# Stacks cleared by VectorE and ScalarE, and the last attention's scores and weighing taken two units at a time

## The reference

```python
# first attention (L0 a), on the layernorm of x: 16 heads of 8, causal
scores = causal_kern[distance] + qm[..., :, None] + km[..., None, :] + 0.15 * (qc @ kc.T) / sqrt(8)
ctx = softmax(where(causal, scores, -1e9)) @ v
...
# last attention (L1 b), on the layernorm of x: 16 heads of 64, one key and value head for all
sim = (q * 64 ** -0.5) @ k.T + rel_emb[bucket(distance)] * 64 ** 0.5      # [4, 16, 1024, 1024]
attn = softmax(where(later_key, -inf, sim))
out = (attn @ v).reshape(4, 1024, 16 * 64) @ Wout + bout
```

## Time and profile before

| what | us |
|---|---|
| median of three runs (3611.07 to 3620.83) | 3611.9 |
| the profiled execution, its own time | 3624.34 |
| its span, first to last instruction | 3622.6 |
| first attention's projection stage, about | 12.8 to 170 |
| last attention's rounds | 2551 to 3371 |
| PE / DVE busy in the span | 3095.8 (85%) / 2363.0 (65%) |

### The profile page before, as it was taken

How to read it: one execution, slowest core, us unless ns; L and a number is a source line. 1 busy time by engine, 2 the same in 40 slices (tenths; PEclk the granted TensorE clock), 3 DMA queues, 4 the chain that set the end, 5 groups by cost and what they waited for, 6 DMA issues and landing times. The chain is left out here.

```text
span 3622.6 us, 67291 instructions
## 1 busy us (share of the span) xinstructions
PE 3095.8 (85%) x25109; PEld 1695.5 (47%) x25109; DVE 2363.0 (65%) x5080; ACT 1838.2 (51%) x3304; POOL 945.5 (26%) x655
## 2 busy tenths in 40 slices
PE   2487999984769999797599978999899999999899
PEld 1223444432347555573222225775355555555676
DVE  2557888872855555564599963225889898889222
ACT  1222666662246233363289962443566666666344
POOL 0004999993100223000000000000222323222100
PEclk8676999997979899896589987999899999999999
DMA  3402333321042000132522210005634334332000
GB/s 82 157 28 66 109 113 114 110 71 35 10 146 94 1 1 1 48 126 77 159 57 69 64 49 19 1 1 181 131 94 104 100 95 104 91 90 73 21 10 12
DMA packets 215996, 264.12 MB, mean 73 GB/s; under 512 B 45243, under 2 KB 164503, under 8 KB 213356
## 3 DMA queue, kind: packets, MB, share of 16 engines
q1 hardware_dynamic: 215709, 260.27, 24.2%
HBM read 204.15 MB, written 56.55 MB: 72 GB/s over the span
## 5 line engine op out<-in xcount | busy, mean ns | idle before, releaser
L1182 POOL TENSOR_TENSOR l0aa_e<-l0aa_e,l0aa_et 128x1024 f32<-128x1024 f32 (+1 forms) x288 | 512.0, 1817 | 46.9 <-ACT l0aa_e L1325 46.9
L2535 ACT ACTIVATE l1ba_sg<-l1ba_sg,l1ba_mn 128x128 f32<-128x128 f32 (+7 forms) x512 | 394.6, 775 | 194.2 <-DVE l1ba_mn L2587 193.1
L2596 DVE STREAM_TRANSPOSE l1ba_pT<-l1ba_sg 128x1024 f32<-128x1024 f32 (+3 forms) x344 | 367.2, 1067 | 42.9 <-PE l1ba_pO L2495 33.0
L2587 DVE CUSTOM_DVE_ANT_0 l1ba_sg<-l1ba_pS,l1ba_tab 128x128 f32<-128x128 f32 (+7 forms) x512 | 368.2, 743 | 34.9 <-PE l1ba_pS L2475 23.1
L1353 DVE TENSOR_REDUCE l0aa_low<-l0aa_pP 128x8 f32<-128x1024 f32 x288 | 343.3, 1220 | 69.9 <-PE l0aa_pP L1206 65.8
L319 PEld LDWEIGHTS f_pY<-l_w,f_hT 128*128 128x128 f32 x2048 | 268.3, 192 | 123.5 <-issue 118.6
L2495 PE MATMUL l1ba_pO<-l1ba_pT,l1ba_v 32*64 32x256 f32 x9216 | 314.3, 387 | 4.6 <-ACT l1ba_y L2550 4.6
L2952 ACT ACTIVATE l1aa_e<-l1aa_e 128x1536 f32<-128x1536 f32 x192 | 284.4, 1483 | 49.1 <-DVE l1aa_e L2993 28.2
L2475 PE MATMUL l1ba_pS<-l1b_k,l1ba_qs 64*128 64x384 f32 (+3 forms) x1024 | 256.6, 581 | 52.1 <-DVE l1ba_mn L2587 38.1
L2423 POOL TENSOR_TENSOR l1ba_co<-l1ba_co,l1ba_rb 128x1024 f32<-128x1024 f32 x64 | 151.4, 2365 | 563.4 <-ACT l1ba_co L2543 492.5
L282 ACT ACTIVATE f_hT<-f_pH,l_b 128x512 f32<-128x512 f32 x256 | 173.9, 687 | 237.4 <-PE f_pH L311 237.2
(11 more groups left out here) (401 smaller groups left out, 5047.4 us busy)
## 6 DMA issues: line engine op xcount, KB each, us to landing
f_wB<-l0f_weights SPq DMA_DIRECT2D x16, 2048.0 KB, 7.1
l1ba_rb<-l1b_rdd SPq DMA_DIRECT2D x64, 512.0 KB
l0aa_et<-l0a_table SPq DMA_DIRECT2D x16, 1536.0 KB, 7.6
l1b_qd<-l1bp_part SPq DMA_DIRECT2D x64, 256.0 KB, 2.3
l1ba_qs<-l1b_qd SPq DMA_DIRECT2D x64, 256.0 KB
l0aa_et<-l0a_table SPq DMA_DIRECT2D x16, 512.0 KB, 8.1
l1ba_tab<-l1b_table SPq DMA_DIRECT2D x32, 256.0 KB, 5.3
l1ba_qs<-l1b_qd SPq DMA_DIRECT2D x64, 128.0 KB
```

Source lines behind the costliest of these rows:

```text
L1182: nc.gpsimd.tensor_tensor(es, es, t, ALU.mult).then_inc(multiplied, heads)
L2535: nc.scalar.activation(row, row, ACT.Exp, bias=mn[:, r % 2, i + k:i + k + 1], scale=-1.0, accum_out=den[:, r % 2, i + k:i + k + 1]).then_i ...
L2587: nc.vector.tensor_tensor_reduce(row, scores, bias, 1.0, 3e38, ALU.add, ALU.min, mn[:, r % 2, h:h + 1]).then_inc(m_done, 1)
L2596: nc.vector.transpose(pT[r % 2][:, i * width(r):(i + heads) * width(r)], sg[:, n % RING, 0:heads * width(r)]).then_inc(t_done, 1)
```

## The change

**At the start.** `fill_stacks` keeps the three transfers of ones and loses the four of zeros. Instead DVE clears rows 32 to 127 of `qs` in the first block (two memsets), ACT copies zeros to rows 32 to 63 of `ks` there and to rows 64 to 127 at the head of the projection's block; SP waits for the latter (`cleared`) before `fill_stacks`. x is loaded in two parts, and the first block doesn't wait for the second. DVE's wait for the weights stands behind the first layernorm (which also waits for `h0_ready`, that PE raises after its own wait for the weights, as before).

**In the last attention.** Nothing but S is due at an even n (counted over all 344 units); at an odd n, behind S(n), stands all that was due at n - 1 and n. The weighing of block 2 moves from the one unit of block 0 to u0' to u2' of the next group, that of block 1 to u3' and u4', that of block 0 to u5' and u6', and the projections of blocks 3, 2 and 1 to u3', u5' and u7'. The turned rows of block 2, 1 and 0 lie side by side in `pT1`, `qs` is used by the parity of the block, and block 7's queries lie in the last seventh of `pT1` (`q7`).

```diff
@@ fill_stacks
-    for dst, name in ((qs[51:54], "minus_ones"), (ks[48:51], "ones"), (ks[MAX_ROWS:MAX_ROWS + 3], "ones"),
-                      (qs[54:MAX_ROWS], "zeros"), (qs[MAX_ROWS + 3:], "zeros"), (ks[54:MAX_ROWS], "zeros"), (ks[MAX_ROWS + 3:], "zeros")):
+    for dst, name in ((qs[51:54], "minus_ones"), (ks[48:51], "ones"), (ks[MAX_ROWS:MAX_ROWS + 3], "ones")):
@@ l0a_project, SP and ACT
+            sp.wait_ge(cleared, 1)
             fill_stacks(sp, D, qs, ks, filled)
...
+            clear_stack(nc, x, ks[64:P]).then_inc(cleared, 1)
             act.wait_ge(w_in, 16 * NW)
@@ attention_strips
+    END = N + 10
+    def turned(r):
+        return {2: (1, 0), 1: (1, 3 * HG * P), 0: (1, 5 * HG * P)}.get(block_of(r), (1 - block_of(r) % 2, 0))
+    def turned_free(r):
+        return r - {7: 3, 6: 1, 1: 2, 0: 5}.get(block_of(r), 1)
+    def next_group(r):
+        return FIRST[r + block_of(r) + 1]
+    def weigh_steps(r):
+        if block_of(r) <= 2:
+            at, steps = {2: (0, 3), 1: (3, 2), 0: (5, 2)}[block_of(r)]
+            return next_group(r) + at, steps
+        return FIRST[r + 1] + 3, FIRST[r + 2] - FIRST[r + 1] - 1
+    def project_step(r):
+        if 1 <= block_of(r) <= 3:
+            return next_group(r) + {3: 3, 2: 5, 1: 7}[block_of(r)]
+        return FIRST[r + 3] + 2 if r + 1 < ROUNDS else N + 8
+    def due(n):
+        return (n - 1, n) if n % 2 else ()
@@ attention_strips, PE (ACT's loop is changed alike)
-            for n in range(FIRST[ROUNDS + 2] + 3):
+            for n in range(END):
                 if n < N:
                     scores(n)
-                for r in range(ROUNDS):
-                    if n == FIRST[r + 3] + 2:
-                        project(r)
-                for r in range(ROUNDS):
-                    first, units = FIRST[r + 1] + 2, FIRST[r + 2] - FIRST[r + 1]
-                    if units > 1:
-                        first, units = first + 1, units - 1
-                    if first <= n < first + units:
-                        weigh(r, (n - first) * pairs(r) // units, (n - first + 1) * pairs(r) // units)
+                for m in due(n):
+                    for r in range(ROUNDS):
+                        if m == project_step(r):
+                            project(r)
+                    for r in range(ROUNDS):
+                        first, units = weigh_steps(r)
+                        if first <= m < first + units:
+                            weigh(r, (m - first) * pairs(r) // units, (m - first + 1) * pairs(r) // units)
```

More of the change, by code:

```diff
@@ L1403, in _, with l0_attn_a @@
                     add_table(n)
-def l0_attn_a(nc, D, x, C, tag, out=None):
+def l0_attn_a(nc, D, x, C, tag, first, out=None):
     with ExitStack() as ctx:
@@ L1550, in _ @@
                 dve.sem_inc(sent[par], 16 * SENDS)
+            layernorm(0, 0)
             dve.wait_ge(w_in, 16 * NW)
-            layernorm(0, 0)
             with dve.Fori(0, BATCH) as b:
@@ L1555, in _ @@
                     g = b * 2 + par
+                    if par:
+                        dve.wait_ge(C["x_rest"], 16)
                     layernorm(g + 1, 1 - par)
@@ L2355, in load_queries @@
             def load_queries(r):
-                if r >= 2:
-                    sp.wait_ge(s_done, FIRST[r - 1])
+                slot = block_of(r) % 2
+                if block_of(r) == U - 1:
+                    if r >= U:
+                        sp.wait_ge(pv_done, r - U + 2)
+                    dst, done = q7, q7_in
+                else:
+                    before = {6: 2, 5: 4}.get(block_of(r), 2)
+                    if r >= U or block_of(r) < 5:
+                        sp.wait_ge(s_done, FIRST[r - before + 1])
+                    dst, done = qs[:, slot], q_in[slot]
                 b, hg = group_of(r)
@@ L2402, in _ @@
                     spread_sums(r - 1)
-                if r + 2 < ROUNDS:
+                if r + 2 < ROUNDS and block_of(r + 2) != U - 1:
                     load_queries(r + 2)
+                if u == 3 and r + 4 < ROUNDS:
+                    load_queries(r + 4)
                 if u == 1 and r + U < ROUNDS:
@@ L2550, in projected @@
                 nc.scalar.activation(y[:, r % 2], pO[BANKS[0]][:, 0:DIM], ACT.Copy).then_inc(y_out, 1)
[L2552 to L2558, removed]
+            for n in range(END):
+                for m in due(n):
+                    for r in range(ROUNDS):
+                        if m == project_step(r):
+                            projected(r)
+                    for r in range(ROUNDS):
+                        if m == out_step(r):
+                            out(r)
                 if n < N:
@@ L3076, in build @@
         C.update(ident=ident, mhalf=mhalf, ident16=ident16, flip=flip)
[L3077 to L3091, removed]
+        C["x_rest"] = ctx.enter_context(nc.semaphore("x_rest"))
@@ new lines, in first, with _ @@
+        def first(qs, ks):
+            with nc.Block() as block:
+                @block.sync
+                def _(sp):
+                    rows = D["x"].rearrange("(b p) d -> p b d", p=P)
+                    sp.dma_start(x[:, GROUP_BLOCKS:3 * GROUP_BLOCKS, :], rows[:, 0:2 * GROUP_BLOCKS, :]).then_inc(loaded, 16)
+                    sp.dma_start(ident[:], D["identity"]).then_inc(loaded, 16)
+                    sp.dma_start(ident16[:], D["identity16"]).then_inc(loaded, 16)
+                    sp.dma_start(flip[:], D["flip"]).then_inc(loaded, 16)
+                    sp.dma_start(x[:, 3 * GROUP_BLOCKS:GROUP_BLOCKS + BLOCKS, :], rows[:, 2 * GROUP_BLOCKS:, :]).then_inc(C["x_rest"], 16)
+                    sp.wait_ge(loaded, 66)
+                @block.scalar
+                def _(act):
+                    act.wait_ge(padded, 1)
+                    clear_stack(nc, x, ks[32:64])
+                @block.vector
+                def _(dve):
+                    nc.vector.memset(x[:, 0:GROUP_BLOCKS, :], 0.0).then_inc(padded, 1)
+                    nc.vector.memset(x[:, GROUP_BLOCKS + BLOCKS:, :], 0.0).then_inc(loaded, 1)
+                    nc.vector.memset(mhalf[:], -0.5).then_inc(loaded, 1)
+                    nc.vector.memset(qs[32:64], 0.0)
+                    nc.vector.memset(qs[64:P], 0.0)
@@ L3092, in build @@
         we = nc.dram_tensor("l0f_weights", (2, 8, GROUP), F32, kind="Internal").ap()
-        l0_attn_a(nc, D, x, C, "l0a")
+        l0_attn_a(nc, D, x, C, "l0a", first)
         with ExitStack() as stages:
```

42 lines of the change are left out of this document (29 added, 13 removed).

## The result

| | before | after |
|---|---|---|
| median of 12 runs, us | 3619.34 (3607.12 to 3632.73) | 3588.28 (3579.71 to 3601.69) |
| profiled execution / its span | 3624.34 / 3622.6 | 3586.44 / 3584.7 |
| first rows of the table stage (`l0at_pU`), behind the projection | 176.3 | 126.0 |
| last rows of the table stage (`l0at_pN`) | 268.6 | 207.7 |
| first scores of the last attention | 2551.3 | 2489.5 |

The ratio is 0.9923, 95% interval 0.9906 to 0.9941: 31 us faster in the medians, not 63. In the two profiles the changed kernel is 50.3 us ahead at the start of the table stage, 60.9 at its end, 61.8 at the last attention, and only 37.9 behind it. The start did what was forecast; the last attention, forecast at -12, took 24 us more (818.7 to 842.6 us from its first scores to its last copy to `y`).

A forecast was written before the change was run, and what follows sets the result against it. It took a start stall behind SP's clears as wholly on the path, and neither DVE nor PE alone as bounding the last attention. 3624.3 - 51 - 12 = 3561 profiled, or 3611.9 - 63 = 3549 us median; range 3515 to 3582.

The forecast's parts named there:

- The start: Up to the projection's end: no stall behind the clears, table load moved, first block longer; -51 us, bounds -40 and -54.
- the last attention, forecast at -12: Whole last attention: -5.5 us at group ends, -8 inside groups, +1.5 for the drain after the last scores.
- Changes of kind: PE in the last attention: 219 fewer switches between kinds of work at 0.19 us each, -41.6 us of PE's time.
- a handover to ACT that S used to cover: PE's uncovered waits in the last attention: 26 more for y at 0.52 us, 29 more for out at 0.70; +33.8 us.
- The walk of the ends: Step-by-step pricing from scores of u42 to lows of u8': even ends 25.0 us (-3.1), odd ends 30.4 (+2.3).
- Inside a group: From u16 to u42: fewer switches of kind against bare handovers; -1.0 us a group, -8 in all, bounds -3 and +1.5.
- The bounds: Last attention: -28 to +8 us with inner bounds alone, -35 to +20 with all ends even-like or odd-like.
- the handovers outweigh it: Last attention: odd ends and pairs with a projection lose 1 us more each, 38 us; 3566 to 3591; chance 0.18.
- The fourth rival: Last attention: the second unit's scores hold PE, DVE waits in each of 172 pairs; slower than before; chance 0.04.
- From the profile to the median: Whole kernel: the profiled execution lies 12.4 us over the median of the runs, so 3561 became 3549 us.

The follow-up runs named there:

- e1: The start of the changed kernel with the last attention of the kernel before: 3563 us, ratio 0.9844 to before.
- e4: The changed kernel with units paired only where neither has a projection, all others unit by unit: 3524 us, ratio 0.9747 to before.
- e6: The changed kernel's PE order (all units paired) with ACT's order from e4: 3575 us, ratio 0.9879 to before.
- e5: The changed kernel's ACT order (all units paired) with PE's order from e4: 3589 us, ratio 0.9924 to before.
- e12: e4 with ACT taking a unit's exponentials ahead of the copies to y and out due at it: 3595 us, ratio 0.9932 to before.
- e2: The changed kernel with the pairing alone undone, the moved weighing kept: 3545 us, ratio 0.9804 to before.
- e9: e4 with the weighing of block 1 whole at u4' and of block 0 whole at u6': 3533 us, ratio 0.9766 to before.
- e10: e4 with POOL's copies of the next group's table rows taken earlier: 3532 us, ratio 0.9757 to before.
- e11: e9 and e10 together, with rows 32 to 63 of qs cleared by POOL instead of DVE: 3506 us, ratio 0.9697 to before.

## Why the prediction was wrong

- **The start: right.** Forecast -51, measured -50.3 at the end of the projection, -55 in e1's median. ACT's group 2 began 50.7 us earlier. In this is that the first layernorm began 2.1 us later (21.70 for 19.56), because two issue gaps of 1.3 us were not in the price of the memsets, and that the table load gave its 1.3 us back. The first block ended near 15, not by 14 us. The rule of the Trainium skill, "VectorE: DVE Perf Modes", section "Zero memsets can be issued as uint32 (trn2)", that zeros go out as words, agrees with the row (6144 for 12288 elements, as the order had shown). Its one cycle per element gave an estimate of 6.4 us; the row has 5.18, and 6.5 with the gap ahead, so that its end at 14.8 is near the 15.0 of the row for another reason than its own.
- **Changes of kind: 28.0 us of the 41.6.** So much less was PE busy in the last attention, where no record is missing. (Over the whole span it was 43.1 us less, 3095.8 to 3052.7, which looks like the forecast by luck: 10.7 of them are the table stage's, which ran at the lower clock for longer before.) In e4, with 452 runs of equal kind for 607, PE was busy 29.8 us less, which is 0.19 for each of 155. The further 64 changes that the changed kernel saves, all at pairs with a projection, brought nothing (730.7 us for e4's 728.8); why is not shown.
- **The failed step: "Against it stands a handover to ACT that S used to cover", at 0.52 and 0.70 us, 33.8 in all.** The count was about right (36 bare handovers to y and 32 to out, of which 32 and 31 were waits), the price was that of an idle ACT. The rows it came from the earlier trace rows stand where nothing was queued ahead of y and out. In a pair the exponential of its first unit is ahead, and at the first even end the eight of u42, where PE stood 2.25 us for y ahead of its W at 2585.12. Measured: 1.18 for an out, 0.77 for a y, 61.2 us in all, 52.3 more than before. So the net of -41.6 + 33.8 = -8 was -28.0 + 51.9 = +24, the idle time being all of PE's.
- **A right price would not have been enough.** e6 has bare handovers at about the forecast's price, 34.4 us in all and 25.5 more than before, and stands 51 us over e4 and 12 over e1 all the same: there ACT waits for PE's later W and P, and DVE for the exponentials behind. e5 and e12 show that ACT's order costs as much without PE's. A sum of PE's waits has no term for either.
- **The walk of the ends** forecast 25.0 and 30.4 us; they took 28.2 to 31.5 and 33.6. The base of 28.05 was also the shortest of before's seven (mean 29.0). In sum +16.9 for -5.5. The walk had ACT's waits in part and POOL's copies not at all.
- **Inside a group** -8 was taken, and +4.9 measured. That was two large terms, not two small ones: e4 against e2 shows pairs without P at -20.2, the changed kernel against e4 those with P at +28.3. The sizes of both, 2.5 and 3.5 us a group, had been taken as under 1.5.
- **The bounds were added up too narrow.** With all ends like the odd ones and +1.5 in each of the eight groups the forecast's own terms give 16.1 + 12 + 1.5 = +30, and with the even ones and -3 they give -44, in place of the +20 and -35 stated. The measured +24 lies outside the latter and inside the former.
- **Which rival.** It was the second, "the handovers outweigh it" (3566 to 3591): it asked for 38 us beyond the walk, and 36 came (+24 for -12). Its reason, each out ahead of an exponential, names the same chain from its other side; e12 shows how large the harm is when the exponential is ahead of the out. That the time itself, 3588, fell into this rival's band is in part luck: two differences that it did not hold, named next, nearly cancel. The fourth rival's mechanism, S of the second unit holding PE, is excluded by e4 for pairs without a projection, which gain.
- **From the profile to the median.** The profiled execution was put 12.4 us over a median of three runs. Over 12 runs it lies 5.0 over, and that of after lies 1.8 under its own. The profile of after came out 25.4 us above the forecast of 3561 (36 in the last attention, less the 10.6 of the table stage); the other 14 of the 39 us are about 12.4 + 1.8, the places of the two profiled executions among their runs.

**The clock inside the groups.** The round of block 6 (from the lows of u8 to the lows of u16) took 16.8 us in some groups and up to 18.9 in others of one kernel, which makes up the 3 to 4 us by which e9 and e10 came out longer inside than e4. The traces show why. Two such rounds of e10, in the second and the fourth group, then the 3.9 us ahead of the clock's fall in the latter, and the time at the lower clock (columns as in the earlier trace rows):

```profile
2610.40:2627.22 16.82, 13.57 (x242) 6.61 (x238) 16.68 (x28) 9.30 (x17) 1.86 (x2) 1.00 0.28 76
2799.49:2818.40 18.91, 15.80 (x232) 7.72 (x236) 16.81 (x27) 9.30 (x17) 1.00 (x2) 0.82 0.19 57
2801.00:2804.90 3.90, 1.69 (x8) 0.30 (x4) 3.76 (x7) 1.96 (x4) 0.00 (x0) 1.00 0.04 8
2804.91:2811.74 6.83, 6.39 (x72) 3.01 (x74) 5.44 (x9) 3.40 (x6) 0.00 (x0) 0.50 0.20 80
```

PE, ahead of DVE, had been busy for 1.69 of 3.90 us; then its clock stood at 1.2 GHz for 6.83 us, in which PE was busy for 6.39 and DVE waited 2.0 us for scores. In e4, e9, e10 and e11 the rounds of block 6 with 6.8 us at the lower clock took 17.6 to 18.9 us, those with none 16.8 to 17.2. So in these rounds, where DVE is otherwise the bound, the lower clock followed a stretch in which PE mostly stood, and made PE the bound for a while.

What stays open: how often the table stage takes its longer time in the kernel before (one trace), and whether it is a draw at all.

## What to carry to other kernels

Putting like work together on one engine saves its changes of kind only where no chain crosses to another engine inside the pair. Before pairing, write down each chain that goes back and forth between engines (here weighing, out, projection, y, weighing), and price each handover with what is then queued ahead of it on the other engine, not from a row in which that engine was idle. A wait also moves when only one of the two engines changes its order, so walk the other engine's queue too. Pair the rest: the whole change with one condition on the pairs (e4) was worth 94 us against before in place of 31. Where an edit removes a wait and the time stays, look for a second thing that ends at the same moment; edits that gain nothing alone may gain together.

## What the runs showed of the hardware

- A memset of zeros over 12288 bf16 elements a row ran as 6144 words in 5.18 us on VectorE, with 1.3 us of issue ahead of each, and as 12288 elements in 10.33 us on GpSimd; VectorE's took the same 5.18 us with GpSimd's beside it and without. ScalarE's copy of zeros took 5.32 us for 6144 float32, less than twelve of its 0.60 us for 512.
- The matrix engine's clock, down since 111 and 112 us, rose from 1.2 to 2.4 GHz at 152 us in one execution and at 173 in another, with the same code up to there; the table stage took 81.7 us in the one and 92.4 in the other.
- After 3.90 us in which the matrix engine was busy for 1.69 its clock stood at 1.2 GHz for 6.83 us, and a round of 16.8 us took 18.9.
